# Second edge stage of a graph network: linear maps that come out edge by edge, and work handed round between VectorE, GpSimd and ScalarE

## What is computed

```
ms = src_s[edge_src] + dst_s[edge_dst];  mv = src_v[edge_src] + dst_v[edge_dst]
w  = (radial network of edge_scalars) @ rw3 + roff                  # five blocks w1..w5
ds = [w1*ms, w4*(mv . Y1)]                                          # 64 + 32 scalars
dv = [(w2*ms) x Y1, w3*mv, w5*cross(mv, Y1)]                        # 64 + 32 + 32 vectors
ls, lv = ds @ lin_ws + lin_bs, dv @ lin_wv                          # 64 + 64 scalars, 32 vectors
a  = sum over 8 of smooth_leaky(ls[:, :64]) * alpha_dot             # one logit a head, 8 heads
a  = exp(a - segment_max(a, edge_dst));  a = a / segment_sum(a, edge_dst)
ns, nv = segment_sum(vs * a), segment_sum(vv * a)                   # by destination
```

## Time and profile before

| what | value |
|---|---|
| median of three runs | 9814.69 us (9813.91 to 9816.08) |
| profiled execution | 9813.87 us, its span 9812.0 us |
| TensorE busy | 8373.1 us (85%) |
| VectorE busy | 7735.9 us (79%) |
| GpSimd busy | 7372.6 us (75%) |
| ScalarE busy | 4874.4 us (50%) |
| second edge stage | about 5330 to 9075 us of the span |

### The profile page before, as it was taken

One profiled execution on the slowest core, in us unless ns is written; L12 is line 12 of the kernel. 1 busy time (PEld: TensorE's weight loads), 2 busy tenths in 40 slices (PEclk: granted clock), 3 DMA queues, 4 the chain that ended last, 5 costly groups with the idle time before them and its releaser, 6 DMA issues. The chain is left out here.

```text
span 9812.0 us, 193495 instructions
## 1 busy us (share of the span) xinstructions
PE 8373.1 (85%) x35878; PEld 5079.2 (52%) x35878; DVE 7735.9 (79%) x14864; ACT 4874.4 (50%) x9073; POOL 7372.6 (75%) x4571
## 2 busy tenths in 40 slices
PE   0788888888888869999985999999999999998588
PEld 0444444444444422222222777777777777777233
DVE  3177777777777768888886999999999999998465
ACT  0176666666666631121121555555555555555355
POOL 4378888888888878778774888888888888886331
PEclk9599999999999989999997999999999999999799
DMA  5578888888888877778773666666666666665222
GB/s 208 180 161 167 167 168 166 167 167 167 167 167 167 167 213 275 267 271 282 264 270 109 136 137 144 137 143 137 144 138 144 138 142 137 144 137 122 59 70 52
DMA packets 1235170, 1618.04 MB, mean 165 GB/s; under 512 B 222610, under 2 KB 1010589, under 8 KB 1178973
## 3 DMA queue, kind: packets, MB, share of 16 engines
q1 hardware_dynamic: 758950, 1273.86, 40.0%
q0 software_dynamic: 475584, 338.58, 27.1%
HBM read 1533.79 MB, written 444.07 MB: 202 GB/s over the span
## 5 line engine op out<-in xcount | busy, mean ns | idle before, releaser
L1952 POOL DMA_INDIRECT e_m<-TS,e_at x1568 | 2631.8, 1678 | 583.7 <-issue 461.4
L442 POOL DMA_INDIRECT sums<-e_total,e_place x1568 | 2506.9, 1599 | 565.9 <-DMA sums<-e_total,e_place 314.5
L579 PE MATMUL ps<-e_win,e_pick 128*128 128x448 f32 x3136 | 1325.8, 568 | 165.0 <-DVE e_u L476 97.0
L579 PEld LDWEIGHTS ps<-e_win,e_pick 128*128 128x128 f32 x3136 | 612.5, 201 | 921.6 <-issue 864.1
L2275 ACT ACTIVATE e_dT<-ps 128x512 f32<-128x512 f32 x1176 | 660.0, 596 | 495.5 <-PE ps L2149 340.1
L2275 ACT ACTIVATE e_oT<-ps 128x512 f32<-128x512 f32 x784 | 468.9, 598 | 615.1 <-PE ps L2177 373.2
L742 DVE SCALAR_TENSOR_TENSOR r_y<-ps,w_rb,r_rstd 128x512 f32<-128x512 f32 x394 | 295.6, 750 | 579.9 <-issue 533.2
L1096 POOL TENSOR_TENSOR n_zv<-n_zv,n_ast 128x1536 f32<-128x1536 f32 x200 | 703.6, 3518 | 36.6 <-DMA n_zv<-in_x_groups 22.5
L1936 POOL TENSOR_TENSOR e_val<-e_val 128x640 f32<-128x640 f32 x392 | 670.9, 1712 | 61.9 <-ACT e_val L2252 61.9
L2018 DVE TENSOR_TENSOR e_q<-e_row,dstI 128x512 f32<-128x512 int32 x392 | 704.2, 1796 | 13.3 <-PE ps L2163 13.3
L711 PE MATMUL ps<-r_sq,w_avg 128*128 128x512 f32 x788 | 458.1, 666 | 277.4 <-issue 277.4
(11 more groups left out here) (448 smaller groups left out, 19299.8 us busy)
## 6 DMA issues: line engine op xcount, KB each, us to landing
e_win<-T SPq DMA_DIRECT2D x1568, 168.0 KB
n_z<-in_x_groups SPq DMA_DIRECT2D x400, 512.0 KB
n_zv<-in_x_groups SPq DMA_DIRECT2D x800, 192.0 KB
TOT<-e_tot SPq DMA_DIRECT2D x392, 352.0 KB, 2.6
e_row<-in_src_rows SPq DMA_DIRECT2D x98, 1024.0 KB
e_local<-LR SPq DMA_DIRECT2D x196, 512.0 KB
e_row<-in_dst_rows SPq DMA_DIRECT2D x98, 1024.0 KB
e_win<-TD SPq DMA_DIRECT2D x1568, 60.0 KB
```

Source lines behind the costliest of these rows:

```text
L442: pool.indirect_dma_start(sums[c], bass.IndirectOffsetOnAxis(ap=place[:, r % 4, c:c + 1], axis=0), total[:, r % 4, c, 0:MSG0], None, compu ...
L579: pe.matmul(g[:, c, :], pick[:, p, R * c:R * c + R], win[:, s, c, :], start=True, stop=True).then_inc(spread, 1)
L1952: pool.indirect_dma_start(m_[:, r % 4, c, :], None, TS, bass.IndirectOffsetOnAxis(ap=at[:, gp, col:col + 1], axis=0), compute_op=ALU.add). ...
```

## The change

1. The maps come out edge by edge. `map_scalars` is four matmuls and `map_vectors` four pairs, each with 128 edges of `dT` as stationary operand and the 128 columns of the weights moving, straight into two PSUM banks of their own. `turn_back`, `oT` and `keep(i, 3)`, `keep(i, 4)` go. `map_scalars` moves up to stand right behind the second transpose, so it waits for `keep(i, 0)`, for the previous step's `results` on ScalarE and for VectorE's first `silued`.
2. `selections` moves from VectorE to ScalarE, as two activations over 128x512: Abs(local - row) and Relu(1 - that). They stand between `keep(i, 1)` and `keep(i, 2)`.
3. `weighted` moves from GpSimd to VectorE, at the head of a step, for step i-7 in place of i-8.
4. `members` is for step i-6 in place of i-5; totals and store are seven behind in place of six.
5. On TensorE `tops_down` stands behind the first totals, `turn(i, 2)` ahead of them; `spread_out`'s halves follow each other. On ScalarE `results` is in its own step, ahead of both `keep_totals`; `weigh_up` comes at the head of the next step. On VectorE `shift` comes behind `weigh`, and in `results` the silu product comes ahead of the vectors.

```diff
         def bank(i, j):
-            return 2 + (7 * i.r + j) % 2
+            return 2 + (5 * i.r + j) % 2
...
@@ GpSimd: weighted(i, 8) goes, the four indirect DMAs stay @@
-                        if not i.before(8):
-                            weighted(i, 8)
...
@@ VectorE, a step @@
+                        if not i.before(7):
+                            weighted(i)
                         if more:
                             sums(after)
                         if r % 4 == 1 and not i.before(5):
                             scans(i)
-                        if i.plus(4).within():
-                            selections(i.plus(4))
                         if not i.before(1):
                             results(i.plus(-1))
+                        if more:
+                            weigh(after)
                         if r % 4 == 1 and not i.before(5):
                             shift(i)
-                        if more:
-                            weigh(after)
-                        if not i.before(5):
+                        if not i.before(6):
                             members(i)
...
@@ TensorE, the maps @@
                 def map_scalars(i):
                     gate(pe, k)
-                    pe.wait_ge(kept, i.n(5, 2))
-                    pe.matmul(ps[:, bank(i, 5), :], W["la"][:].rearrange("u a h x -> u (a h x)"), dT[:, 0, :], start=True, stop=True
-                              ).then_inc(turned, 1)
+                    pe.wait_ge(kept, i.n(3, 1))
+                    if not i.before(1):
+                        gate(pe, k)
+                        pe.wait_ge(outs, i.n(2))
+                        gate(pe, k)
+                        pe.wait_ge(silued, i.n(2, -1))
+                    for c in range(GT):
+                        last = pe.matmul(scalar_out4[:, c], dT[:, 0, R * c:R * c + R],
+                                         W["la"][:].rearrange("u a h x -> u (a h x)"), start=True, stop=True)
+                    last.then_inc(mapped, 1)
...
@@ TensorE, a step @@
                         if i.plus(3).within():
-                            spread_out(i.plus(3), 0, far2(i, 0), (far_kept, 5) if i.before(1) else (kept, i.n(5, -1)))
-                        if not i.before(1):
-                            turn_back(i.plus(-1), 0)
-                        if i.plus(3).within():
-                            spread_out(i.plus(3), 1, far2(i, 1), (far_kept, 6) if i.before(1) else (kept, i.n(5)))
-                        if not i.before(1):
-                            turn_back(i.plus(-1), 1)
+                            spread_out(i.plus(3), 0, far2(i, 0), (far_kept, 5) if i.before(1) else (kept, i.n(3, -1)))
+                            spread_out(i.plus(3), 1, far2(i, 1), (far_kept, 6) if i.before(1) else (kept, i.n(3)))
...
                         turn(i, 0)
                         turn(i, 1)
-                        if not i.before(6):
+                        map_scalars(i)
+                        turn(i, 2)
+                        if not i.before(7):
                             totals(i, 0)
-                        turn(i, 2)
                         if r % 4 == 1 and not i.before(5):
                             tops_down(i)
-                        map_scalars(i)
-                        if not i.before(6):
+                        map_vectors(i)
+                        if not i.before(7):
                             totals(i, 1)
-                        map_vectors(i)
...
@@ ScalarE @@
+                def selections(i):
...
+                    act.activation(pick[:, p, :], local[:, gp, GT * R * s:GT * R * s + GT * R], ACT.Abs, bias=minus[:, 0:1]
+                                   ).then_inc(distant, 1)
+                    gate(act, k)
+                    act.wait_ge(distant, i.n(1, 1))
+                    act.activation(pick[:, p, :], pick[:, p, :], ACT.Relu, bias=one[:, 0:1], scale=-1.0).then_inc(picked, 1)
...
-                        if not i.before(1):
-                            results(i.plus(-1))
+                        if r % 4 == 2 and not i.before(6):
+                            weigh_up(i.plus(-1))
                         keep(i, 0)
                         keep(i, 1)
-                        if not i.before(6):
+                        if i.plus(4).within():
+                            selections(i.plus(4))
+                        keep(i, 2)
+                        results(i)
+                        if not i.before(7):
                             keep_totals(i, 0)
-                        keep(i, 2)
-                        keep(i, 3)
-                        if not i.before(6):
                             keep_totals(i, 1)
-                        if r % 4 == 1 and not i.before(5):
-                            weigh_up(i)
-                        keep(i, 4)
```

More of the change, by code:

```diff
@@ L1921, in _ @@
                 passes(sp, body)
-                for r in range(6):
-                    store(At(PASSES, r), 6)
+                for r in range(7):
+                    store(At(PASSES, r), 7)
                 for s in range(STEPS):
@@ L1928, in _ @@
             def _(pool):
[L1929 to L1937, removed]
                 def body(t):
@@ L2108, in _ @@
                 shift(At(PASSES, 0))
-                for r in range(5):
+                for r in range(6):
+                    weighted(At(PASSES, r))
                     members(At(PASSES, r))
+                weighted(At(PASSES, 6))
             @block.tensor
@@ L2146, in turn @@
                     else:
-                        pe.wait_ge(kept, i.n(5, j - 1))
+                        pe.wait_ge(kept, i.n(3, j - 1))
                     for c in range(GT):
@@ L2152, in totals @@
                 def totals(i, half):
-                    j = i.r - 6
+                    j = i.r - 7
                     slot = j % STEPS
                     gate(pe, k)
-                    pe.wait_ge(u_ready, i.n(1, 1, 6))
+                    pe.wait_ge(u_ready, i.n(1, 1, 7))
                     gate(pe, k)
-                    pe.wait_ge(q_ready, i.n(1, 1, 6))
-                    if not (i.before(7) and half == 0):
+                    pe.wait_ge(q_ready, i.n(1, 1, 7))
+                    if not (i.before(8) and half == 0):
                         gate(pe, k)
-                        pe.wait_ge(totkept, i.n(2, half, 6))
+                        pe.wait_ge(totkept, i.n(2, half, 7))
                     for c in (2 * half, 2 * half + 1):
@@ L2237, in _ @@
                 passes(pe, body)
-                for j in range(2):
-                    turn_back(At(PASSES - 1, STEPS - 1), j)
                 logits_up(At(PASSES, 0))
                 tops_down(At(PASSES, 0))
-                for r in range(6):
+                for r in range(7):
                     for half in range(2):
@@ L2273, in keep @@
                         act.wait_ge(mapped, i.n(2))
-                    to = dT[:, j, :] if j < 3 else oT[:, j - 3, :]
-                    act.activation(to, ps[:, bank(i, 2 + j), :], ACT.Copy).then_inc(kept, 1)
+                    act.activation(dT[:, j, :], ps[:, bank(i, 2 + j), :], ACT.Copy).then_inc(kept, 1)
                 def keep_totals(i, half):
-                    j = i.r - 6
+                    j = i.r - 7
                     slot = j % STEPS
                     gate(act, k)
-                    act.wait_ge(summed, i.n(2, half + 1, 6))
-                    if not i.before(14):
+                    act.wait_ge(summed, i.n(2, half + 1, 7))
+                    if not i.before(15):
                         gate(act, k)
@@ L2324, in _ @@
                         keep_far(At(0, r), half, far2(At(0, 0), half))
+                    if r < 2:
+                        selections(At(0, r + 2))
                 passes(act, body)
-                results(At(PASSES - 1, STEPS - 1))
                 weigh_up(At(PASSES, 1))
-                for r in range(6):
+                for r in range(7):
                     for half in range(2):
```

95 lines of the change are left out of this document (51 added, 44 removed).

## The result

The changed kernel takes 9918.24 us (median of 4 runs, 9909.42 to 9921.4) against 9814.3 before, a ratio of 1.0099 (95% interval 1.008 to 1.0118). The forecast was 9660, with a range of 9520 to 9790. The profiled execution took 9915.85 us, its span is 9914.1.

The account below looks back on a forecast made before the run. TensorE was taken as the bound of clean steps, with 7.2 us a pass lost waiting on VectorE. Forecast pass: 8 x 8.72 + 0.3 + 1.7 + 0.4 = 72.2 us against 75.3, times 49 saves 152: 9660 us, range 9520 to 9790.

Parts of the forecast that it names:

- the SyncE queue: Windows behind the store: hidden in a plain step, at a pass's start 1.7 us stall plus 0.4 for the clock.
- VectorE: Second edge stage: `members` falls to 0.60 us, `weighted` adds 0.74 start to start, 8.4 us a step in all.
- Clean step: TensorE's step from spread to spread goes from 8.51 to 8.72 us, between 8.58 and 8.92.
- my price of the old maps: TensorE: six 512-wide map passes put at 2.57 us a step; 24 short ones at 0.1 more, 2.67.
- the stalls: TensorE waits for ScalarE's copies ahead of `map_scalars`, 0.54 us, and ahead of `map_vectors`, 0.45 us, each step.
- ScalarE: `selections` as two activations of 0.69 us fits into idle time but for 0 to 0.15 us; 0.04 taken.
- Rival 2: Weight loads of the 24 map passes show; gain gone from 0.127 us a pass; 9920 to 10530 us; chance 0.06.
- Rival 3: VectorE stays late, `members` keeping 1.8 us for another reason (int32 input); 9815 to 9890 us; chance 0.04.
- Rival 4: TensorE's 1.0 us of stall a step brings the 1.2 GHz clock level, 1.7 us a step; 10330 us; chance 0.03.
- Rival 1: SyncE's queue holds up nothing and maps stream at 0.107 us a pass; 69.3 us a pass, 9520 us; chance 0.20.
- my case: Stage limited by TensorE's chain with some stall at the pass's start; 9590 to 9740 us; chance 0.55.
- What would show me wrong: A clean step over 9.2 us, VectorE busy without a gap, or windows late in every step.

Follow-up runs that it names:

- c1: a1 with SyncE's `load_row` one step later as well; 9550.77 us, 0.9764 of the kernel before.
- a1: The changed kernel with SyncE's store one step later (eight behind in place of seven); 9591.55 us, 0.9797 of the kernel before.
- a2: The changed kernel with `load_h` ahead of `load_windows` in SyncE's queue; 9810.7 us, 1.001 of the kernel before.
- c2: The changed kernel with only `load_row` one step later, store as changed; 9830.81 us, 1.0047 of the kernel before.
- a4: The changed kernel with the maps in their old form (`turn_back`, `oT`, five `keep`), the rest as changed; 9843.93 us, 1.0054 of the kernel before.
- b1: a4 with the store one step later; 9627.35 us, 0.9822 of the kernel before.
- c3: b1 with `load_row` one step later; 9450.25 us, 0.9658 of the kernel before.
- c4: b4 with `load_row` one step later and `selections` moved back ahead of `results` on ScalarE; 9391.7 us, 0.9602 of the kernel before.
- a3: The changed kernel with `weighted` back on GpSimd for step i-8, the rest as changed; 9909.3 us, 1.0119 of the kernel before.
- b4: Changed kernel: totals in TensorE's two stalls, `selections` last on ScalarE, store one step later, `load_h` ahead of windows; 9651.55 us, 0.9835 of before.

## Why the prediction was wrong

**The step that failed** is the last term, the SyncE queue: "In a plain step ... hidden", and 1.7 + 0.4 us a pass at its start. Without that term the forecast pass was 72.2 - 2.1 = 70.1 us. With both waits of the queue asked for a step older (c1), where no load is late, the pass is 8 x 8.79 = 70.3. In the changed kernel it is 77.3. So all other terms together were right to 0.2 us (partly by luck, see the clean step below), and the queue costs 7.0 us where 2.1 were put: 4.9 more a pass, 240 us over 49, nearly the whole miss of 258. Of the 7.0, 5.2 are TensorE's waits for the queue's loads: 1.5 for windows, where 1.7 were put, and 3.7 for `e_h`, where nothing was put. The rest was not split; the slow clock is in it, for which 0.4 was put.

What the term left out:
- It followed one load, the windows. The queue also carries `load_h` behind them, used in the same step of TensorE 1.1 us after the spread, and `load_local` ahead of it every fourth step. The windows' wait at the pass's start was right (1.67 us against 1.7); the waits for `e_h` were not in the sum, and some two thirds of them (97.4 of 142.9 us) are for the `e_h` behind `e_local`.
- It followed one wait, the store's. `load_row`'s wait was not changed, and by that became a step tighter when `members` went to i-6. It is not in the diff.
- It looked for a late load at the pass's start alone, where the queue loses 5 us (store at 7493.21, first window at 7498.20). a1 leaves the loop's end and the loads as they are, and takes away more than the stall there. The other waits come one and five steps later, where `e_local` goes ahead of `e_h`. Whether the queue is still late there from the pass's start, or each step's wait for the last totals is enough with 512 KB ahead, no run separates.

That the store's wait holds the loads up is shown by a1 (one line, TensorE's program unchanged); that the order of the loads alone gives back less than a third of that, by a2; that the row's load is the rest, by c1 and c2 (its wait or its place). Why the store's wait got later is read from the timelines: the last totals are kept 3.5 us behind the transposes before, 4.4 with `selections` on ScalarE (a4), 6.3 to 6.6 with `totals(i, 1)` behind `map_vectors` as well. That lateness the forecast had right; what it made late behind it was wrong. With the old maps too both edits were needed: by the ratios a4 to b1 is 228 us for the store, b1 to c3 161 us for the row.

**The other steps.**
- *VectorE*: right. `members` 0.68, `weighted` 0.82; the step's busy time is 969.81 x 8.38 / 1000 = 8.1 us in c4, against 8.4 from start to start. a3 supports the cause: with the multiplication on GpSimd the excess is there again, on other lines. The Trainium skill, "SBUF — State Buffer", section "Who interferes with whom", gives the rule of two SBUF inputs, and `e_cr` and `members` agree with it; `e_mask`, with one tensor input, went from 0.27 to 1.02 us as well, which the two inputs don't explain. The same section lists `tensor_scalar`, which this is, among the operations that can take both ports; whether it did so here no run shows.
- *Clean step*: 8.68 to 8.98 against 8.72, and 8.79 in the mean of c1. Its parts were off, and cancel: that the sum came out is in part luck. `map_scalars` takes 1.0 us and `map_vectors` 1.89, 0.12 a pass and 0.32 above my price of the old maps where I took 0.1; the stalls were 0.25 to 0.60 (a mean of 0.37 a step) and 0.17 in a third of the steps with none listed in the others, where I took 0.54 and 0.45.
- *ScalarE*: the two activations of `selections` take 0.72 each, against 0.69.
- *Rival 2*, weight loads that show, decided at 0.127 us a pass. It was 0.12. The rule that the prediction took from the Trainium skill ("TensorE: Matmul & The Clock Gate", "The mechanism"), that loads overlap only in other row groups, would have made it 0.21 by my estimate, and these passes contradict it again. The section itself also lets a load into the background weight buffer go ahead, which the prediction left out and which would agree.
- *Rival 3* fell with the changed kernel's own row of `members`, 0.68 with the int32 input as before. *Rival 4* fell with c1, which has both stalls and a granted clock of 1.00 from 6000 to 8000; after has 0.99, with the slow spells behind the longer waits for loads. *Rival 1* was wrong in the same place as my case.
- *What would show me wrong*: neither a clean step over 9.2, nor VectorE without a gap; the third, late windows in more than one step, nearly: in steps other than the pass's first it was their neighbour in the queue.

The expected gain was there: c1, with SyncE's two edits, has it (0.9764, where the forecast was 9660 / 9814 = 0.984), and with the totals in the stalls it is more (c4, 0.9602). It was lost in the queue.

**Open:** the kernel before was run with a later store, not with a later row too, so what the change brings apart from the queue is bounded, not measured. What weighting on VectorE is worth with a free queue wasn't tried, nor c4's two edits over b4 apart, nor the two things that the row's edit does.

## What to carry to other kernels

When a step is moved, list every wait in every queue on what it produces, the untouched ones above all: a count "six behind" that was free can be this step's. In a queue in order a wait delays all the loads behind it, each with its own deadline, so follow every one of them, with what large transfer goes ahead of it, and not only the first. The time for which a queue stands is not the loss: c1's stands for 309 us of 2800 and loses none. And when a load was issued late, move the wait that stood ahead of it; moving the load (a2) helped less and made another one late.

## What the runs showed of the hardware

- The excess that GpSimd's multiplication causes on VectorE is not a property of one line: with the order in time changed it falls on others. With `weighted` on GpSimd `e_cr` went from 548 to 933 ns, and the 127 wide `e_mask` from 266 to 1021.
- `e_h`, 128 KB, was used 3.1 us after its issue by an engine that had waited for it (7502.42 to 7505.50), and 5.1 us after when 512 KB had been issued just ahead of it (7510.33 to 7515.44). From 6000 to 7200 it was 2.6 to 3.3 us in 20 waits of the first kind and 4.4 to 5.8 in 26 of the second.
- 24 fp32 passes with 128 columns, each with a weight load of its own, ran at 0.12 us a pass (1.00 + 1.89 us in the changed kernel), where the same columns in passes of 512 are put at 0.107 by the prediction's estimate.
- TensorE's `weights` took 1.68 us in a clean step and 3.2 to 3.4 at its slowest, behind waits for loads (6024.37, granted clock 0.86 around it), and no step of c1, with stalls of some 0.4 us, was slow.
